# A macaron block with routed feed-forward: the class arithmetic of its sort moved to GpSimd, the sort's steps dealt out evenly over the tiles, and the counting matmuls put behind the last pair

## The chip, the cores and the metric

The kernel runs on one core of a Trainium2 chip. The metric is the device time of one execution in microseconds (us). Engines are named as the profile names them: PE (TensorE), ACT (ScalarE), DVE (VectorE), POOL (GpSimd), SP (SyncE, which here only starts transfers). PEld is the weight load of a matmul.

## The reference

The block is feed-forward, recurrence, feed-forward, each added to its input (cut to what matters):

```python
x = x + 0.5 * ffn(layernorm(x), W1, b1, W2, b2)
x = x + mixer(layernorm(x), W_toP, ..., W_fromP)      # projections and a scan over t
x = x + 0.5 * ffn(layernorm(x), W1, b1, W2, b2)

def ffn(x, W1, b1, W2, b2):                           # 8 experts, hidden 128 -> 512 -> 128
    h = mod(x[:, :2].sum(axis=1).astype(int32), 8)    # the class of a row
    for e in range(8):
        w = ((h == e) | (mod(h + 1, 8) == e)) / 2
        acc += w[:, None] * (maximum(x @ W1[e] + b1[e], 0) @ W2[e] + b2[e])
```

x has 16 sequences of 512 rows with 128 columns in float32, so 8192 rows. Each row uses two neighbouring experts, given by its class.

## The kernel before

**Tiles.** A feed-forward pass sorts the 8192 rows by class and works in 36 tiles of 256 rows, each gathered from DRAM by two indirect transfers (POOL, line 575) and scattered back by two (line 583). A *pure* tile holds one class; a *mixed* tile has two halves with classes of their own. `layout(j)` gives the order: `LEAD` pure tiles first, then mixed and pure by turns. Per tile PE does layer 1 (lines 877 to 879, each product as high and low halves in float16) and layer 2 (lines 895 and 897) of the tile before; ACT makes the high halves (`hhi`, line 703; `xhi`, line 709); DVE makes the low halves (`hlo`, line 1423, twice; `xlo`, line 1417), adds the bias row to the gathered rows (`residual`, line 1437, two instructions) and collects the result (`collect`, lines 1444 and 1447). PE's layer 1 of the next tile waits for that tile's `xlo`.

**The sort in two parts.** So that tiles can begin early, the first 48 of 64 row columns are sorted ahead of the pass and the last 16 inside it, between the tiles. Each part runs on DVE: row statistics (`bn_stats`), `moments` and `class_sum`, `classify` (a one-hot `oh` per class), then `count` on PE (lines 817 and 818), `ranks`, `assign_first` or `assign_rest` (arithmetic on 8 numbers, one per class, that ends in `code8`; `look_up` spreads it to the rows), `one_hots`, `select` on PE (line 831, 16 matmuls a group), `route` (writes `places`, the gather's indices) and `tables`. Inside a pass the helper `between(j, STEPS, ...)` takes up to 6 steps of the sort at two places of each tile, after the first `hlo` and after `collect`; a step ends at a `yield`. A stage must be done by its last tile (`all_of_it`).

**The order of the work.** Every engine runs its own list in the order written; semaphores join them. SP starts the loads in the order X (6 chunks), W1, W2, b2, `rows` (normalised rows for the gather), X (2 chunks), b1. Ahead of the first pass, PE and ACT also scale and split the 8 experts' W1 (`w_times` line 805, `w_less` line 810, `w_high`, `w_low`) and ACT sums the squares of W2 (line 686); the scale found from that goes through POOL back to ACT (line 692). The mixer runs over 8 pairs of sequences `q`; `add_out(q)` (line 1514) adds its result to X and takes the statistics of the new rows (line 1493). In its loop, at `q == NPAIR - 2`, DVE runs `own_classes(2)` and `classify(0, 48)` for the second pass, and PE has `count(3, ...)` there.

Of the kernel before, what the change touches and what calls it, by code (L numbers as in the profile page):

```python
# [22 lines left out]
P = 128  # L23
# [3 lines left out]
def macaron_kernel(nc, x, W_toP, W_U, W_F, W_V, W_lam, B_mat, C_mat, W_fromP, W1, b1, W2, b2, out):  # L27
# [17 lines left out]
    LEAD = PURE - (MIXED - 1)  # L45
# [10 lines left out]
    EARLY = 6  # L56
# [7 lines left out]
    with ExitStack() as ctx:  # L64
# [77 lines left out]
        n8 = sb("n8", [P, E])  # L142
        n8_i = sb("n8_i", [P, E], I32)
        p8 = sb("p8", [P, E])
        w8 = sb("w8", [P, E])
        u8 = sb("u8", [P, E])
        whole1 = sb("whole1", [P, E + 1])
        whole2 = sb("whole2", [P, E + 1])
        parts = sb("parts", [P, E + 1])
        code8 = sb("code8", [P, E])  # L150
# [73 lines left out]
        b1_hi = sem("b1_hi")  # L224
# [214 lines left out]
        STEPS = 6  # L439
        COUNT_AT = (3, 3)  # L440
        SELECT_AT = ((6, 7, 8, 9), (6, 7, 8, 9))

        @block.sync
        def _(sp):
# [7 lines left out]
            sp.dma_start(w1r[:], W1.rearrange("e d f -> d e f")).then_inc(w_in[0], 16)  # L452
            sp.dma_start(w2r[:], W2.rearrange("e (c p) d -> p e c d", p=P)).then_inc(w_in[2], 16)
# [10 lines left out]
            for c in range(FIRST[0] // XC, NX):  # L464
                load_x(c)
# [25 lines left out]
        def _(pool):  # L491
# [52 lines left out]
            pool.wait_ge(b1_hi, 2)  # L544
            g.tensor_tensor(b1l[:], b1f[:], b1h[:], ALU.subtract).then_inc(b1_lo, 1)
            pool.wait_ge(sum_in, 2)
# [82 lines left out]
        def _(act):  # L629
# [39 lines left out]
            nc.scalar.activation(b1h[:], b1r[:], ACT.Identity, scale=scl[0:E, 0:1]).then_inc(b1_hi, 1)  # L669
            nc.scalar.activation(b1f[:], b1r[:], ACT.Identity, scale=scl[0:E, 0:1]).then_inc(b1_hi, 1)  # L670
# [111 lines left out]
        def _(pe):  # L782
# [54 lines left out]
            def first_sort():  # L837
# [4 lines left out]
                warm(8, 0)  # L842
# [5 lines left out]
                w_less(EARLY - 2)  # L848
                w_less(EARLY - 1)
                for g in range(FIRST[0] // GRP):  # L850
                    if g == FIRST[0] // GRP - 1:
                        pe.wait_ge(sq_done, 2)
                        nc.tensor.matmul(ps[:, 6, 2:3], ones[:], sq[:, 2:3], start=True, stop=True,
                                         skip_group_check=True).then_inc(sum_pe, 1)
                    select(0, g)
# [746 lines left out]
```

## Time and profile before

| what | value |
|---|---|
| median of 3 runs | 618.48 us (616.67 to 619.98) |
| the profiled execution's own time | 618.32 us |
| its span | 616.5 us |
| PE busy | 522.9 us (85%) |
| DVE busy | 457.2 us (74%) |
| POOL busy | 314.5 us (51%) |
| ACT busy | 296.2 us (48%) |
| chain that ended last | PE 61%, DVE 22%, ACT 6% |

Read the table from the top: the profiled execution lies within the runs, 1.8 us of its time lie outside the span, and no engine is busy throughout. The stages have different limits: the head (0 to 54 us), the first pass (54 to 273), the mixer (273 to 361) and the second sort ahead of its pass (361 to 389), the second pass (389 to 608).

### The profile page before, as it was taken

Reading aid. Unit: us, or ns where it says so; the run is one execution under the profiler, and the core shown is the slowest. Engines: PE = TensorE matmul, PEld = TensorE weight load, DVE = VectorE, ACT = ScalarE, POOL = GpSimd, SP = SyncE. Lnnn points to the kernel's source line nnn. Section 1 sums busy time; section 2 is a strip of 40 time slices with the busy share of each in tenths; the row PEclk is TensorE's granted clock in tenths of the full one; section 3 lists DMA queues with packets and bytes.
Section 4 is the critical chain, followed back from the end, with each engine's and each line's share of the span. In section 5 each row is a group of like instructions: output and inputs, shape, how many; then the busy total and the mean of one; then the engine's idle time right before and its main releaser. Section 6 shows DMA issues by size and latency. Waiting matters only on the chain.

```text
span 616.5 us, 16284 instructions
## 1 busy us (share of the span) xinstructions
PE 522.9 (85%) x5367; PEld 441.8 (72%) x5367; DVE 457.2 (74%) x1191; ACT 296.2 (48%) x494; POOL 314.5 (51%) x379
## 2 busy tenths in 40 slices
PE   0586996999999999965799388798799999999991
PEld 0243885998999999952466264587698999999981
DVE  6887898778777777756876659589778777777771
ACT  2585352445555555522988110554344555555540
POOL 3128263647777767640016201646365777777642
PEclk9978898999999999997999787999899999999996
DMA  9961211112221112109003510241011221112200
GB/s 244 351 221 41 92 41 31 36 36 48 54 46 50 45 37 55 45 21 250 23 2 70 120 19 5 49 97 45 27 42 35 54 54 47 50 43 44 47 31 10
DMA packets 37852, 40.99 MB, mean 66 GB/s; under 512 B 5813, under 2 KB 30731, under 8 KB 37266
## 3 DMA queue, kind: packets, MB, share of 16 engines
q1 hardware_dynamic: 27698, 21.65, 12.7%
q0 software_dynamic: 9088, 17.87, 11.4%
q8 instruction: 52, 0.85, 0.6%
q10 hardware_dynamic: 992, 0.44, 0.3%
q14 instruction: 22, 0.18, 0.1%
HBM read 23.00 MB, written 17.83 MB: 66 GB/s over the span
## 4 chain that ended last, share of the span: by engine, by line
PE 61%; DVE 22%; ACT 6%; issue 4%; DMA 3%; SPq 1%; POOL 1%; DVEq 1%; POOLq 0%; ACTq 0%
PE ps L895 16%; PE ps L877 9%; PE ps L879 9%; PE ps L878 9%; PE ps L897 8%; DVE hlo L1423 5%; PE ps L913 2%; PE ps L797 2%; PE ps L831 2%; ACT hhi L703 2%; DVE bn L1493 1%; DMA X<-in_L_attn_x 1%; SPq L447 1%; DVE X L1514 1%; DMA X<-x1d 1%
## 5 line engine op out<-in xcount | busy, mean ns | idle before, releaser
L703 ACT ACTIVATE hhi<-ps 128x1024 f16<-128x1024 f32 x144 | 145.8, 1013 | 208.4 <-PE ps L879 208.4
L1423 DVE SCALAR_TENSOR_TENSOR hlo<-ps,hhi 128x1024 f16<-128x1024 f32 x144 | 173.9, 1208 | 85.8 <-ACT hhi L703 85.6
L575 POOL DMA_INDIRECT G<-rows,places x142 | 141.7, 998 | 133.2 <-PE ps L879 47.7
L895 PE MATMUL ps<-w2s,hhi 128*128 x1136 | 203.8, 274 | 0.1
L897 PE MATMUL ps<-w2s,hlo 128*128 x1136 | 196.1, 220 | 0.0
L877 PE MATMUL ps<-xhi,w1s 128*128 128x128 f16 (+1 forms) x736 | 169.9, 251 | 23.1 <-DVE xlo L1417 21.9
L879 PE MATMUL ps<-xhi,w1s 128*128 128x128 f16 (+1 forms) x736 | 169.7, 251 | 0.0
L878 PE MATMUL ps<-xlo,w1s 128*128 128x128 f16 (+1 forms) x736 | 169.6, 251 | 0.0
L895 PEld LDWEIGHTS ps<-w2s,hhi 128*128 128x128 f16 x1136 | 111.7, 98 | 12.6 <-issue 0.2
L897 PEld LDWEIGHTS ps<-w2s,hlo 128*128 128x128 f16 x1136 | 111.7, 98 | 1.4
L877 PEld LDWEIGHTS ps<-xhi,w1s 128*128 x736 | 72.6, 99 | 33.3 <-issue 27.7
L583 POOL DMA_INDIRECT x1d<-O,places x71 | 72.2, 1017 | 37.8 <-issue 22.7
L583 POOL DMA_INDIRECT out<-O,places x71 | 72.1, 1015 | 38.0 <-issue 24.7
L879 PEld LDWEIGHTS ps<-xhi,w1s 128*128 x736 | 72.6, 99 | 5.5
L717 ACT ACTIVATE xn<-G 128x127 f32<-128x127 f32 x142 | 62.0, 490 | 29.9 <-DMA G<-rows,places 29.9
L878 PEld LDWEIGHTS ps<-xlo,w1s 128*128 x736 | 72.7, 99 | 3.7
L797 PE MATMUL ps<-ones_row,ones 128*128 128x512 f16 x109 | 31.9, 457 | 10.2 <-DMA X<-x1d 9.5
L1437 DVE TENSOR_TENSOR O<-G,b2t 128x128 f32<-128x128 f32 x142 | 34.9, 286 | 2.6 <-issue 2.2
L1444 DVE SCALAR_TENSOR_TENSOR O<-ps,scl_i,O 128x256 f32<-128x256 f32 x72 | 33.9, 471 | 3.7 <-PE ps L897 3.7
L1447 DVE SCALAR_TENSOR_TENSOR O<-ps,scl_i,O 128x256 f32<-128x256 f32 x72 | 34.6, 480 | 2.5
L1417 DVE TENSOR_TENSOR xlo<-ps,xhi 128x256 f16<-128x256 f32 x72 | 29.6, 411 | 6.9 <-ACT xhi L709 6.9
L797 PEld LDWEIGHTS ps<-ones_row,ones 128*128 128x128 f16 x109 | 12.2, 115 | 26.6 <-issue 18.3
(263 smaller groups left out, 539.8 us busy)
## 6 DMA issues: line engine op xcount, KB each, us to landing
rows<-X SPq DMA_DIRECT2D x5, 1040.0 KB, 7.0
X<-in_L_attn_x SPq DMA_DIRECT2D x8, 512.0 KB, 8.7
X<-x1d SPq DMA_DIRECT2D x8, 512.0 KB, 7.2
rows<-X SPq DMA_DIRECT2D x1, 3120.0 KB, 12.7
G<-rows,places POOLq DMA_INDIRECT x142, 2.6
w1r<-in_L_ffn_W SPq DMA_DIRECT2D x1, 2048.0 KB, 9.0
x1d<-O,places POOLq DMA_INDIRECT x71, 2.3
out<-O,places POOLq DMA_INDIRECT x71, 2.3
```

The costliest lines, as they stand in the source:

```text
L575: nc.gpsimd.indirect_dma_start(out=G[tile.slot][:, s, :], out_offset=None, in_=src, in_offset=bass.IndirectOffsetOnAxis(ap=places[:, tile. ...
L583: nc.gpsimd.indirect_dma_start(out=dst, out_offset=bass.IndirectOffsetOnAxis(ap=places[:, tile.at, SUB + s:SUB + s + 1], axis=0), in_=O[ti ...
L703: nc.scalar.activation(hhi[tile.k][e][:, :, 0:tile.cols], H[e][:, :, 0:tile.cols], ACT.Relu).then_inc(hi_done[e], 1)
L717: ins = nc.scalar.activation(xn[tile.k][:, s, 0:D - 1], g[:, s, 0:D - 1], ACT.Identity, bias=g[:, s, D:D + 1], scale=g[:, s, D + 1:D + 2])
L797: nc.tensor.matmul(ps[:, bank, :], ones16[:], ones_row[:], start=True, stop=True)
L877: nc.tensor.matmul(o, hi, xhi[tile.k][:, tok], start=True, stop=False)
L878: nc.tensor.matmul(o, hi, xlo[tile.k][:, tok], start=False, stop=False)
L879: ins = nc.tensor.matmul(o, lo, xhi[tile.k][:, tok], start=False, stop=True)
L895: nc.tensor.matmul(Y[tile.k][:, s, :], hhi[tile.k][e][:, c, tok], w, start=first, stop=False, skip_group_check=True)
L897: ins = nc.tensor.matmul(Y[tile.k][:, s, 0:P], hlo[tile.k][e][:, c, tok], wh, start=False, stop=(e == 1 and c == CH - 1), skip_group_check ...
L1423: v.scalar_tensor_tensor(out=hlo[tile.k][e][:, :, c], in0=H[e][:, :, c], scalar=0.0, in1=hhi[tile.k][e][:, :, c], op0=ALU.max, op1=ALU.sub ...
L1437: ins = v.tensor_tensor(O[tile.slot][:, s, :], G[tile.slot][:, s, 0:D], b2v[:, bass.ds(at[0 if tile.pure else s], D)], ALU.add)
```

## The change

- `assign_first` and `assign_rest` lose their arithmetic on 8 classes. POOL does it (`codes_first`, `codes_rest`) with the scan over classes replaced by three shifted additions; DVE signals `counted` and waits for `coded` ahead of `look_up`. In a pass, `codes_rest` stands in POOL's list ahead of the gather of tile 6 + 4 (first pass) or 5 + 4 (second).
- Steps carry a cost (`yield 4`); `between` deals 4 units at each of the two places of a tile and carries what is over. The last part of the sort is spread over more tiles: counting after tile 4 or 3 as before 3, all four `select` groups after tile 12 or 11, where they stood after tiles 7 to 10, one each. 17 pure tiles lead, not 15. The second half's one-hot of the rank (`slots_of`) is made before the codes are there.
- Statistics of the last 16 columns move: 11 of 16 in the first sort ahead of the pass; those of the mixer's last two pairs out of `add_out`, 12 behind `tables` and 4 behind the first `xlo`.
- In the mixer `classify(0, 48)` runs behind the scan of the last pair, and `count(3, ...)` stands behind PE's loop.
- In the head, X's last two chunks are loaded ahead of W2; W1's 8 experts are all split ahead of the last `select`; POOL scales b1 and adds b2 earlier; `warm` has 6 matmuls, not 8.
- `residual` of a pure tile is one instruction.

```diff
-    LEAD = PURE - (MIXED - 1)
+    LATE = "MPMPMMPMPMPMMPMPMPM"
+    LEAD = NJ - len(LATE)
-    EARLY = 6
+    EARLY = 4
...
-        STEPS = 6
-        COUNT_AT = (3, 3)
-        SELECT_AT = ((6, 7, 8, 9), (6, 7, 8, 9))
+        STEPS = 4, 4
+        COUNT_AT = (4, 3)
+        CODES_AT = (6, 5)
+        SELECT_AT = (12, 11)
...
             sp.dma_start(w1r[:], W1.rearrange("e d f -> d e f")).then_inc(w_in[0], 16)
+            for c in range(FIRST[0] // XC, NX):
+                load_x(c)
             sp.dma_start(w2r[:], W2.rearrange("e (c p) d -> p e c d", p=P)).then_inc(w_in[2], 16)
...
             sp.dma_start(*rows_of(0, FIRST[0])).then_inc(rows_first[0], 16)
-            for c in range(FIRST[0] // XC, NX):
-                load_x(c)
...
+            def whole_of(out, src, less, by):
+                link(g.tensor_scalar(k8[:, 0], src, less, by, ALU.add, ALU.mult))
+                link(g.tensor_scalar(out, k8[:, 0], ROUND, -ROUND, ALU.add, ALU.add))
+            def summed(out, src):
+                link(g.tensor_tensor(z[3][:, own], src[:, own], src[:, after], ALU.add))
+                link(g.tensor_tensor(z[4][:, own], z[3][:, own], z[3][:, E - 2:2 * E - 2], ALU.add))
+                link(g.tensor_tensor(out[:, own], z[4][:, own], z[4][:, E - 4:2 * E - 4], ALU.add))
+            def codes_first(r):
+                pool.wait_ge(counted, 1 + 2 * r)
+                whole_of(z[5][:, own], n8[:, 0], 0.5 - FT / 2, 1.0 / FT)
+                summed(z[0], z[5])
...
+                g.tensor_tensor(code8[:, 0], k8[:, 3], k8[:, 2], ALU.add).then_inc(coded, 1)
+            def codes_rest(r):
+                pool.wait_ge(counted, 2 + 2 * r)
...
+                g.tensor_tensor(code8[:, 1], k8[:, 9], k8[:, 6], ALU.add).then_inc(coded, 1)
+            codes_first(0)
...
                 for j in range(NJ):
                     tile = Tile(r, j)
+                    if j == CODES_AT[r]:
+                        codes_rest(r)
...
+            w_both(0, EARLY)
             act.wait_ge(w_in[2], 16)
             nc.scalar.activation(w2s[:, :, :, 0:P], w2r[:], ACT.Square, accum_out=sq[:, 2:3]).then_inc(sq_done, 1)
+            w_both(EARLY, E - 2)
             act.wait_ge(sum_pe, 2)
             nc.scalar.activation(sums[:, 2:3], ps[:, 6, 2:3], ACT.Copy).then_inc(sum_in, 1)
+            w_both(E - 2, E)
             act.wait_ge(scale_ready, 2)
...
                 if q >= 1:
                     out_s(q - 1)
-                if q == NPAIR - 2:
-                    count(3, 0, FIRST[1])
+            count(3, 0, FIRST[1])
             out_x(NPAIR - 1)
...
+                dve.wait_ge(coded, 2 + 2 * r)
+                yield from look_up(1, NT)
...
-                stages = [(0, COUNT_AT[r] - 1, rest_classes(r)), (COUNT_AT[r] + 1, min(SELECT_AT[r]) - 1, rest_ranks(r))]
-                stages += [(SELECT_AT[r][g], SELECT_AT[r][g], one_hots(2 * r + 1, g)) for g in range(NT // GRP)]
-                stages += [(max(SELECT_AT[r]) + 2, max(SELECT_AT[r]) + 3, rest_routes(r))]
+                stages = [(0, COUNT_AT[r] - 1, early_part()), (COUNT_AT[r] + 1, SELECT_AT[r] - 1, middle_part()),
+                          (SELECT_AT[r] + 1, REST_AT[r] - 1, rest_routes(r))]
+                owed = [0.0]
                 def between(j, n, all_of_it):
                     for start, end, steps in stages:
                         if start <= j <= end:
-                            for k, _ in enumerate(steps):
-                                if k + 1 >= n and not (all_of_it and j == end):
+                            owed[0] += n
+                            while owed[0] > 0 or (all_of_it and j == end):
+                                cost = next(steps, -1)
+                                if cost == -1:
+                                    owed[0] = min(owed[0], 0.0)
                                     break
+                                owed[0] -= cost or 1
...
+                    if q >= NPAIR - 2:
+                        continue
                     if tiles is None:
                         dve.wait_ge(mx2, 2 * q + h + 1)
                         all_of(stats3(q, h))
...
+                if q == NPAIR - 1:
+                    run(classify(0, FIRST[1]))
...
-                    run(classify(0, FIRST[1]))
             run(ranks(3, 0, FIRST[1]))
+            run(slots_of(2, 0))
             run(assign_first(1))
```

Where the order of instructions moves, at three places. First, PE at the mixer's last pair: lines 817/818 (now 870/871) are the count of the second sort, lines 988 to 997 (now 1044 to 1053) the last pair's products. Before:

```order
L973 MATMUL ps<-m,w1r 128x128 x8
L817 MATMUL ps<-oh,after 128x384
L818 MATMUL ps<-oh,ones 128x384
L988 MATMUL ps<-w2r,wA 128x512
L989 MATMUL ps<-w2r,wB 128x512
L964 MATMUL ps<-m,w2r 128x128 x8
L997 MATMUL ps<-w1r,wL 128x512
```

With the change, the same place of PE's list:

```order
L1044 MATMUL ps<-w2r,wA 128x512
L1045 MATMUL ps<-w2r,wB 128x512
L1020 MATMUL ps<-m,w2r 128x128 x8
L1053 MATMUL ps<-w1r,wL 128x512
L1029 MATMUL ps<-m,w1r 128x128 x8
L870 MATMUL ps<-oh,after 128x384
L871 MATMUL ps<-oh,ones 128x384
```

The count has moved from ahead of the last pair's products to behind them.

Second, DVE in the first pass, from one `xlo` to the first `hlo` behind it, in the tile that follows the count. Before:

```order
L1106 SCALAR_TENSOR_TENSOR cum<-fresh,ps 128x128
L1111 TENSOR_TENSOR posv<-cum,ps 128x128
L1117 TENSOR_TENSOR posv<-posv,n 128x128
L1120 TENSOR_TENSOR n<-n,cum 128x8
L1121 TENSOR_TENSOR posv<-posv,oh 128x128
L1124 TENSOR_REDUCE rank<-posv 128x16
L1127 CAST q_i<-rank 128x16
L1417 TENSOR_TENSOR xlo<-ps,xhi 128x256
L321 TENSOR_LOAD tab_b
L1437 ISA
L1437 TENSOR_TENSOR O<-G,b2t 128x128 x2
L1423 SCALAR_TENSOR_TENSOR hlo<-ps,hhi 128x1024
```

With the change:

```order
L1159 SCALAR_TENSOR_TENSOR cum<-fresh,ps 128x128
L1167 TENSOR_TENSOR n<-n,cum 128x8
L1168 TENSOR_TENSOR posv<-cum,ps 128x128
L1417 TENSOR_TENSOR xlo<-ps,xhi 128x256
L321 TENSOR_LOAD tab_b
L1437 ISA
L1437 TENSOR_TENSOR O<-G,b2t 128x256
L1423 SCALAR_TENSOR_TENSOR hlo<-ps,hhi 128x1024
```

Three instructions of the sort stand ahead of `xlo` where seven stood, and the class totals `n`, for which POOL waits, come second.

Third, PE in the head: line 805 (now 858) scales an expert of W1, line 810 (now 863) takes its low half, line 831 (now 884) selects rows for the gather, line 853 (now 907) sums W2's squares. Before:

```order
L810 MATMUL ps<-w1s,minus 128x512 x3
L831 MATMUL ps<-onehot_a,onehot_b 128x34 x32
L853 MATMUL ps<-sq,ones 128x1
L831 MATMUL ps<-onehot_a,onehot_b 128x34 x16
L805 MATMUL ps<-w1r,fold 128x512 x2
L810 MATMUL ps<-w1s,minus 128x512 x2
L797 MATMUL ps<-ones_row,ones 128x512 x12
```

With the change:

```order
L884 MATMUL ps<-onehot_a,onehot_b 128x34 x16
L863 MATMUL ps<-w1s,minus 128x512
L907 MATMUL ps<-sq,ones 128x1
L863 MATMUL ps<-w1s,minus 128x512
L858 MATMUL ps<-w1r,fold 128x512 x2
L884 MATMUL ps<-onehot_a,onehot_b 128x34 x16
L863 MATMUL ps<-w1s,minus 128x512 x2
L884 MATMUL ps<-onehot_a,onehot_b 128x34 x16
L850 MATMUL ps<-ones_row,ones 128x512 x12
```

The last group of the selection now stands behind the last experts of W1, not ahead of them.

## Rows read from the trace of the kernel before

**Rows 1.** Page, costliest groups: busy, mean ns of one | idle before, releaser.
```profile
L877 PE MATMUL ps<-xhi,w1s 128*128 128x128 f16 (+1 forms) x736 | 169.9, 251 | 23.1 <-DVE xlo L1417 21.9
```

**Rows 2.** DVE timeline, `xlo` of single tiles: start, us, instruction.
```profile
54.13 0.42 DVE L1417 TENSOR_TENSOR xlo<-ps,xhi 128x256 f16<-128x256 f32 x1 [3.45 <-ACT xhi L709]
...
154.43 0.41 DVE L1417 TENSOR_TENSOR xlo<-ps,xhi 128x256 f16<-128x256 f32 x1
...
159.94 0.41 DVE L1417 TENSOR_TENSOR xlo<-ps,xhi 128x256 f16<-128x256 f32 x1
...
388.88 0.42 DVE L1417 TENSOR_TENSOR xlo<-ps,xhi 128x256 f16<-128x256 f32 x1 [3.48 <-ACT xhi L709]
...
485.42 0.41 DVE L1417 TENSOR_TENSOR xlo<-ps,xhi 128x256 f16<-128x256 f32 x1
```

**Rows 3.** Windows: us, busy of PE, PEld, DVE, ACT, POOL; PE clock; DMA share; GB/s.
```profile
154.43:159.94 5.51, 5.51 (x80) 5.25 (x79) 4.06 (x9) 3.08 (x5) 4.21 (x5) 1.00 0.20 52
87.19:94.02 6.83, 5.66 (x58) 4.89 (x58) 6.27 (x23) 3.08 (x5) 4.51 (x5) 1.00 0.17 47
40.00:45.00 5.00, 3.76 (x21) 2.69 (x22) 2.49 (x7) 3.42 (x5) 2.55 (x7) 0.50 0.06 13
```

**Rows 4.** Chain that ended last, 70 to 125 us: one group of the selection.
```profile
111.71 1.21 PE ps L831 x16
```

**Rows 5.** DVE timeline, first pass: first and last operation of `assign_rest`'s class arithmetic.
```profile
90.72 0.29 DVE L1195 CAST n_i<-n 128x8 int32<-128x8 f32 x1
...
98.09 0.17 DVE L1243 SCALAR_TENSOR_TENSOR code<-p,n 128x8 f32<-128x8 f32 x1
```

**Rows 6.** POOL and DVE timelines: small operations on POOL, one beside a DVE scan.
```profile
334.34 0.22 POOL L346 TENSOR_TENSOR l_v<-l_y,l_b 128x16 f32<-128x16 f32 x1
334.65 0.26 POOL L344 TENSOR_SCALAR l_c<-l_c 128x16 f32<-128x16 f32 x1
...
321.40 1.24 POOL L344 TENSOR_SCALAR l_c<-l_c 128x16 f32<-128x16 f32 x1
...
321.38 1.22 DVE L1549 TENSOR_TENSOR_SCAN w1r<-w1r 128x512 f32<-128x512 f32 x1
```

**Rows 7.** PE timeline at the mixer's last pair.
```profile
341.53 1.16 PE L973 MATMUL ps<-m,w1r 64*128 64x128 f32 x16
352.85 0.50 PE L817 MATMUL ps<-oh,after 128*128 128x384 f16 x1 [10.16 <-DVE oh L1098]
```

**Rows 8.** DVE timeline from there to the second pass's gather indices.
```profile
346.66 0.18 DVE L353 TENSOR_TENSOR l_m<-bn 128x16 f32<-128x16 f32 x1
...
350.73 0.19 DVE L1077 TENSOR_SCALAR c_b<-cls_s 128x48 f32<-128x48 f32 x1
...
360.35 1.23 DVE L1549 TENSOR_TENSOR_SCAN w1r<-w1r 128x512 f32<-128x512 f32 x1 [7.56 <-ACT w1r L775]
...
362.19 0.87 DVE L1493 BATCH_NORM_STATS2 bn<-X 128x6 f32<-128x128 f32 x4
...
364.48 0.93 DVE L1106 TENSOR_TENSOR_SCAN cum<-fresh,ps 128x384 f32<-128x384 f16 x1
```

**Rows 9.** POOL, ACT and PE timelines at the second pass's start.
```profile
382.78 1.30 POOL L575 DMA_INDIRECT G<-rows,places  x1 [38.62 <-DVE places L1307]
...
387.00 0.88 ACT L717 ACTIVATE xn<-G 128x127 f32<-128x127 f32 x2 [26.68 <-DMA G<-rows,places]
...
379.19 7.80 PE L797 MATMUL ps<-ones_row,ones 128*128 128x512 f16 x24
```

**Rows 10.** ACT, PE and POOL timelines in the head.
```profile
37.48 3.62 ACT L686 ACTIVATE w2s<-w2r 128x4096 f16<-128x4096 f32 x1
...
42.79 3.67 PE L805 MATMUL ps<-w1r,fold 128*128 128x512 f32 x4
...
46.26 1.23 POOL L575 DMA_INDIRECT G<-rows,places  x1 [0.18 <-issue]
```

More of the change, by code:

```diff
@@ L141, in macaron_kernel @@
         gone = sb("gone", [P, NT])
[L142 to L150, printed above, removed]
+        n8 = sb("n8", [P, 2, E])
+        k8 = sb("k8", [P, 12, E])
+        z16 = sb("z16", [P, 7, 2 * E])
+        whole1, whole2, parts = (z16[:, i, E - 1:2 * E] for i in range(3))
+        code8 = sb("code8", [P, 2, E])
         pairs8 = sb("pairs8", [P, E])
@@ L542, in _ @@
             power(c1).then_inc(scale_ready, 1)
-            pool.wait_ge(b1_hi, 2)
+            ROUND = 1.5 * 2.0 ** 23
+            z = [z16[:, i, :] for i in range(7)]
+            own, after = slice(E, 2 * E), slice(E - 1, 2 * E - 1)
+            def whole_of(out, src, less, by):
[5 more added lines that the diff above has]
+                link(g.tensor_tensor(out[:, own], z[4][:, own], z[4][:, E - 4:2 * E - 4], ALU.add))
@@ L1238, in assign_rest @@
-                yield
-                ch.wait()
-                ch.mark(v.tensor_tensor(n8[:], n8[:], u8[:], ALU.add))
-                yield
-                ch.wait()
-                ch.mark(v.scalar_tensor_tensor(out=code8[:], in0=p8[:], scalar=16384.0, in1=n8[:], op0=ALU.mult, op1=ALU.add))
-                yield
-                ch.wait()
-                yield from look_up(NT)
+                s = slice(0, FIRST[r])
+                dve.wait_ge(coded, 2 + 2 * r)
+                yield from look_up(1, NT)
@@ L1392, in rest_ranks @@
                 yield from ranks(2 + 2 * r, FIRST[r], NT)
+                for g in range(NT // GRP):
+                    yield from slots_of(2 * r + 1, g)
                 yield from assign_rest(r)
@@ L1397, in rest_routes, with some @@
                 yield from tables(2 * r + 1)
+            def some(steps, n):
+                for cost in steps:
+                    n -= cost or 1
+                    if n <= 0:
+                        break
+            late_stats = [rest_stats(0), rest_stats(1)]
             run(classify(0, FIRST[0]))
+            some(late_stats[0], 4)
             run(ranks(1, 0, FIRST[0]))
+            dve.wait_ge(iota_ready, 1)
+            run(slots_of(0, 0))
             run(assign_first(0))
-            dve.wait_ge(iota_ready, 1)
-            for g in range(FIRST[0] // GRP):
+            run(one_hots(0, 0))
+            for g in range(1, FIRST[0] // GRP):
+                run(slots_of(0, g))
                 run(one_hots(0, g))
+            some(late_stats[0], 11)
             run(route(0))
@@ L1576, in _ @@
             run(tables(2))
+            some(late_stats[1], 16)
             ffn(1)
```

251 lines of the change are left out of this document (112 added, 139 removed).

## The prediction

> **What bounds the kernel now.** I began with the page's groups of instructions, because they say what each engine waited for. PE is busy 85% of the span; its largest wait is the one ahead of layer 1 for `xlo` on DVE, 21.9 us in all [rows 1]. Next I took the start of single `xlo` instructions from DVE's timeline, which dates the tiles [rows 2]. Without steps of the sort a tile takes 159.94 - 154.43 = 5.51 us, and there PE is busy 5.51 of 5.51 us, DVE 4.06, POOL 4.21 [rows 2, 3]: the pass is bound by PE. The first 15 tiles are not. They take 154.43 - 54.13 = 100.30 us in the first pass and 485.42 - 388.88 = 96.54 in the second, against 15 x 5.51 = 82.65 [rows 2]. A tile that holds 12 sort steps takes 6.83 us, and DVE is busy 6.27 of them [rows 3]: there DVE is the bound. Last, the timelines at the mixer's end. PE finishes a product at 342.7 and then stands for 10.16 us, because the count is next in its list and waits for the one-hot `oh` of `classify` on DVE; the last pair's products stand behind that count [rows 7]. So the kernel has three places where PE waits for DVE: early tiles of both passes, and the mixer's end.
>
> 0.5% of this time is 3.1 us, about what a measurement of this kernel can tell from no change. The sum is made against the profiled execution, 618.32 us (616.5 in the span), 0.16 under the median.
>
> **(a) The mixer's end and the second sort: -11.8 us.** Before, DVE ends `own_classes` at 350.73, where `classify` begins, and `classify` runs until PE's count at 352.85, so 2.12 us [rows 7, 8]. The scan of the last pair then starts only at 360.35, 7.5 us behind, since PE and ACT make its input after the count; with two additions to X and 8 row statistics (two of 4, about 0.81 each) `ranks` starts at 364.48 [rows 8]. With the change PE goes on at 342.7, and the same 7.5 us put the scan's input at about 350.2, before DVE is through with `own_classes`. DVE then does the scan (1.23), `classify` (2.12) and the two additions (364.48 - 360.35 - 1.14 - 1.62 = 1.37): 350.73 + 4.72 = 355.45 instead of 364.48, so -9.0. From `ranks` to the gather it was 382.78 - 364.48 = 18.30 us [rows 8, 9]. Out of that go 8 class operations of about 0.19 (1.5 us) and the other 8 statistics (1.6 us); the moved ones are dealt behind `tables` and the first `xlo`, where PE is warming or working. That is -12.1, if POOL's answer is in time: 10 operations at a pitch of 0.31 (334.65 - 334.34) are 3.1 us [rows 6], and DVE has 3.7 us of its own ahead of `look_up` (the positions, the rank and one one-hot). The gather's landing 4.2 us later is not alone: PE's 24 warming matmuls end at 379.19 + 7.80 = 386.99, as `xn` starts at 387.00 [rows 9]. Both move with the selection; I give back 0.3 for a slower clock in the warming. Bounds: -12.6, and -10 if warming takes 2 us longer.
>
> **(b) First 15 tiles of the second pass: -7.1 us.** What PE cannot avoid is 82.65, plus four groups of selection at 1.21 each [rows 4], 4.85. The rest depends on DVE. In a tile with 12 steps, 6.83 - 4.06 = 2.77 us go to the steps, 0.23 a step [rows 3]. The change deals 8 units a tile: 8 x 0.23 + 4.06, less about 0.1 for the single `residual`, gives 5.8 against 5.51, 0.3 late. I count about 93 units in the list, 11.6 tiles, so 3.5 us a pass, at most 4.2 with slips; and none if DVE's lead in the two tiles without steps absorbs it. I take 2.3, past the middle, since 0.3 us is 5% of a tile and the cost of a step is a mean. The first interval is 0.4 shorter by fewer statistics in it. 82.65 + 4.85 + 2.3 - 0.4 = 89.4 against 96.54.
>
> What makes the steps fewer is the class arithmetic, which leaves DVE: 18 operations from 90.72 to 98.09, 0.16 to 0.29 each, 3.4 us a pass [rows 5]. On POOL it is 22 operations, 19 linked, 19 x 0.31 + 3 x 0.22 = 6.5 us. DVE asks for it some 12 units, 1.45 tiles, after it gave the totals: 8.0 us of cover. The gathers behind it in POOL's list are 6.5 us late; they stand four tiles ahead (22 us), land within 4.2, and POOL wins back 5.51 - 4.21 = 1.30 a tile [rows 3], so nothing waits for them.
>
> **(c) First 15 tiles of the first pass: -9.7 us.** The same 82.65 + 4.85 + 2.3. Three statistics stand ahead of the second `xlo` where twelve stood (-0.6). PE comes out of the head at a granted clock of 0.50 [rows 3], the lower of its two levels (1.2 of 2.4 GHz), with fewer warming matmuls; for that I add 1.4, a quarter of a tile, between 0 and 2.8. 90.6 against 100.30.
>
> **(d) The head: +1.5 us.** The last group of the selection moves behind four scaling matmuls of experts 6 and 7, which took 3.67 us at the lower clock [rows 3, 10]. With their low halves the route, and the gather that stood at 46.26, come up to 3 us later; at the full clock they come at the same time. ACT's sum of squares (37.48, 3.62 us [rows 10]) starts earlier, as it no longer waits for the split of two experts; X's two chunks ahead of W2 delay its landing, still under that start. DVE leaves its part of the critical path. Bounds -0.9 and +3. POOL's work on b1 and b2 lies ahead of the route, which it used to follow: nothing.
>
> Sum: -11.8 - 7.1 - 9.7 + 1.5 = -27.1, so **591.2 us**.
>
> **The rivals.**
> *Codes come late.* POOL's prices are from a quiet stretch. Beside a DVE scan the same operation took 1.24 us instead of 0.26 and ended with it [rows 6]. If the mix costs 0.6 an operation, 22 x 0.6 = 13.2 less 8.0 leaves 5.2 late in each pass, and PE, with DVE late by as much, follows: 591.2 + 10.4 = 601.6. The Trainium skill, page "SBUF — State Buffer", section "Who interferes with whom", states that GpSimd shares a port pair with DVE's second input under an exclusive lock, so that one waits until the other's instruction ends. The trace agrees, 1.24 beside a scan of 1.22 [rows 6]. By it I would put the 6.5 us at about 9.0, 1.0 late a pass, and the time at 593. Chance 0.12.
>
> *The class arithmetic on POOL becomes the bound* (the other side). At 1.24 us for every operation [rows 6] 22 take 27.3, 19.3 past the cover, twice 38.6; and the 10 ahead of each pass 12.4, 8.7 past their cover in the second: about 638. Against it: DVE's steps of 0.2 to 0.5 us are mostly shorter than that scan, and it is idle a quarter of the time. It decides from about 0.98 us an operation, where 2 x (22 x 0.98 - 8.0) = 27.1. Chance 0.05, of which 0.02 near no change.
>
> *The spreading does nothing*: DVE's work is the same, each pass is as late as before, and only (a) and (d) remain: 618.3 - 11.8 + 1.5 = 608. For it: PE waits for whatever is late last. Against it: DVE's total in 15 tiles, 15 x 4.0 + 93 x 0.23 = 81, is under PE's 87.5. Chance 0.05.
>
> *Half of the mixer's gain* if DVE, busy in the whole of PE's gap [rows 7, 8], receives the scan's input later than 350.7: 597. Chance 0.08.
>
> **How the numbers follow.** The forecast has 0.70. Its own best end (no lag, full clock, head -0.9) is about 583, its worst (lag 4.2 twice, head +3, mixer -10) about 598. The late codes take the range to 602; outside lie the spread's rival (0.05), the slower one (0.05), the part of the late codes beyond 0.6 an operation (about 0.05) and a tail of the forecast, below 0.2 in all. Faster by over 0.5%: 0.95; within: 0.02; slower: 0.03.
>
> **What would show it.** (a) PE's wait of 10.16 ahead of the count is gone, `ranks` starts near 355.5 plus the shift of the passes, and from the last pair's end to the first `xlo` it is 12 us less. (b, c) The wait for `xlo` falls from 21.9 to about 5, and `xlo` intervals in the first 15 tiles are 5.5 to 6.0. POOL's class operations show 0.2 to 0.3 us and DVE's `look_up` does not wait for them. (d) The first `xlo` is at about 55.6. It is wrong if `look_up` waits for POOL, if PE waits for `xlo` just as long, or if tiles 9 to 12 wait for gathers.

## The result, and the profile after

The changed kernel takes 594.51 us (median of 4 runs, 593.97 to 595.11); beside it the kernel before took 619.23 us. The ratio is 0.9608, with a 95% interval of 0.9576 to 0.9640. The forecast was 591.2 us in a range of 583 to 602: the sign is right, the time lies in the range, and the gain is 24.4 us (profiled execution 593.97 against 618.32) where 27.1 were forecast.

The span went from 616.5 to 592.0 us. First the same group of the page as [rows 1], with its new line number: busy, mean ns of one | idle before, releaser.

```profile
L933 PE MATMUL ps<-xhi,w1s 128*128 128x256 f16 (+1 forms) x736 | 171.3, 251 | 6.2 <-DVE xlo L1417 4.8
```

PE's wait for `xlo` fell from 21.9 to 4.8 us. To date the stages, DVE's timeline of the changed kernel (start, us, instruction): the first `xlo` of each pass, the sixteenth, and the last.

```profile
55.30 0.42 DVE L1417 TENSOR_TENSOR xlo<-ps,xhi 128x256 f16<-128x256 f32 x1 [1.99 <-ACT xhi L762]
...
145.75 0.41 DVE L1417 TENSOR_TENSOR xlo<-ps,xhi 128x256 f16<-128x256 f32 x1
...
257.29 0.28 DVE L1417 TENSOR_TENSOR xlo<-ps,xhi 128x128 f16<-128x128 f32 x1
...
369.56 0.42 DVE L1417 TENSOR_TENSOR xlo<-ps,xhi 128x256 f16<-128x256 f32 x1 [1.25 <-ACT xhi L762]
...
458.94 0.42 DVE L1417 TENSOR_TENSOR xlo<-ps,xhi 128x256 f16<-128x256 f32 x1
...
571.17 0.28 DVE L1417 TENSOR_TENSOR xlo<-ps,xhi 128x128 f16<-128x128 f32 x1
```

The kernel before has its first and sixteenth in [rows 2]; its last of each pass are these:

```profile
264.68 0.28 DVE L1417 TENSOR_TENSOR xlo<-ps,xhi 128x128 f16<-128x128 f32 x1
...
595.64 0.28 DVE L1417 TENSOR_TENSOR xlo<-ps,xhi 128x128 f16<-128x128 f32 x1
```

Differences between these starts give the whole account:

| stretch | before | after | change | forecast |
|---|---|---|---|---|
| (d) head, to the first `xlo` | 54.13 | 55.30 | +1.2 | +1.5 |
| (c) first 15 tiles, pass 1 | 100.30 | 90.45 | -9.9 | -9.7 |
| the other 20 tiles of pass 1 | 110.25 | 111.54 | +1.3 | none |
| (a) last `xlo` to the next pass's first | 124.20 | 112.27 | -11.9 | -11.8 |
| (b) first 15 tiles, pass 2 | 96.54 | 89.38 | -7.2 | -7.1 |
| the other 20 tiles of pass 2 | 110.22 | 112.23 | +2.0 | none |

The four terms that were forecast came out within 0.3 us each. That is closer than executions agree: two kernels below whose instructions are the same up to tile 17 (`mixed_run` and `fixed_addr`) have their first `xlo` at 55.04 and 55.73 us and take 91.52 and 91.94 us for the first 15 tiles of the first pass. What is missing is a stretch that had no term: the tiles behind the sixteenth, where the kernel before ran at 5.51 us a tile. Two windows there, columns as in [rows 3]: from the `xlo` of tile 22 of the first pass to that of tile 23, and on to that of tile 24.

```profile
183.04:188.84 5.80, 5.80 (x82) 5.39 (x79) 4.06 (x9) 3.08 (x5) 4.28 (x6) 1.00 0.17 50
188.84:195.19 6.35, 6.28 (x69) 5.43 (x68) 4.05 (x9) 3.08 (x5) 4.01 (x5) 1.00 0.12 34
```

They are 5.80 and 6.35 us at the full clock (2.4 GHz), with DVE busy for no more than 4.06 us, as in a tile of 5.51. The next two intervals are 5.57 and 5.62, so 1.3 us are lost. The same happens seven tiles on and at both places of the second pass, four times 1.3 = 5.2 us. These are the two places in `LATE` with "MM", two mixed tiles side by side (21 and 22, 28 and 29); the alternation before had none. (The rows of the table show less, 3.3, since `xlo` had fallen behind PE during the selection and makes that up there: the two intervals behind tile 15 of the first pass are 4.84 and 4.90 us; in the second pass one is short, 5.00.)

One more loss lies inside the first 15 tiles, and no term had it. Before, the selection stood behind four tiles, 16 matmuls (128x37) each; now all 64 stand in a row. Windows, columns as in [rows 3]: the kernel before over its four groups of the first pass, then the changed kernel at the end of the row in the first and in the second pass.

```profile
110.00:135.00 25.00, 25.00 (x280) 23.31 (x278) 18.21 (x33) 10.94 (x17) 14.90 (x15) 1.00 0.15 41
```

```profile
130.00:135.00 5.00, 5.00 (x54) 4.47 (x52) 0.41 (x1) 0.00 (x0) 3.78 (x5) 0.75 0.19 53
440.00:445.00 5.00, 5.00 (x38) 4.07 (x36) 0.07 (x1) 1.12 (x2) 3.98 (x4) 0.50 0.19 53
```

PE's granted clock falls from 1.00 to 0.75 and 0.50 there, though PE shows as busy. The tile behind the row takes PE 6.91 and 8.09 us from its first product of layer 1 to the next tile's (133.18 to 140.09 and 441.10 to 449.19), where the tiles shortly ahead take 5.48: 1.4 and 2.6 us. It varies between executions: in the second pass of `b2_later` (experiment 8) the same tile took 5.66 us at a clock of 1.00. No run deals the four groups out again, so what that would bring is not shown.

The mixer's end, on PE and DVE, with the first gather on POOL:

```profile
340.34 1.16 PE L1029 MATMUL ps<-m,w1r 64*128 64x128 f32 x16
346.69 0.50 PE L870 MATMUL ps<-oh,after 128*128 128x384 f16 x1 [5.19 <-DVE oh L1151]
...
347.87 0.95 DVE L1159 TENSOR_TENSOR_SCAN cum<-fresh,ps 128x384 f32<-128x384 f16 x1
...
363.50 1.32 POOL L625 DMA_INDIRECT G<-rows,places  x1 [10.27 <-DVE places L1291]
```

From the last `xlo` to `ranks` it is now 347.87 - 257.29 = 90.58 us, before 364.48 - 264.68 = 99.80 [rows 8]: -9.2, forecast -9.0. From `ranks` to the gather 15.63 against 18.30: -2.7, forecast -3.1. PE still waits 5.19 us for the one-hot `oh`, but only the last pair's products of the output stand behind it; the scan's input is made ahead.

The class arithmetic in the first pass: its first, its longest and its last operation on POOL, and DVE beside it.

```profile
91.80 0.26 POOL L551 TENSOR_SCALAR k<-n 128x8 f32<-128x8 f32 x1
...
97.47 1.24 POOL L587 TENSOR_SCALAR k<-k 128x8 f32<-128x8 f32 x1
...
99.08 0.20 POOL L590 TENSOR_TENSOR code<-k 128x8 f32<-128x8 f32 x1
...
97.42 1.23 DVE L1266 TENSOR_TENSOR onehot_b<-iota_rep,b_h 128x2048 f16<-128x2048 f16 x1
98.56 1.22 DVE L1423 SCALAR_TENSOR_TENSOR hlo<-ps,hhi 128x1024 f16<-128x1024 f32 x1
99.70 0.68 DVE L1194 TENSOR_TENSOR posv<-oh,code 128x512 f32<-128x512 f16 x1
```

POOL takes 7.5 us (91.80 to 99.28), one operation being stretched to 1.24 beside a DVE instruction of 1.23, as in [rows 6]. DVE takes up `look_up` at 99.70 and waits for nothing, with 0.4 us to spare.

### The profile page after: what moved, and what is told of

It reads as the page before. It is cut to its first block, busy times and chain, and to the rows that moved or that the text cites. A ratio compares the mean times of both kernels' runs of the same rounds, so it can differ in the third digit from the quotient of the medians.

```text
span 592.0 us, 16239 instructions
## 1 busy us (share of the span) xinstructions
PE 521.4 (88%) x5365; PEld 441.6 (75%) x5365; DVE 443.8 (75%) x1087; ACT 296.1 (50%) x492; POOL 339.1 (57%) x445
## 3 DMA queue, kind: packets, MB, share of 16 engines
q0 software_dynamic: 9088, 17.87, 11.3%
## 4 chain that ended last, share of the span: by engine, by line
PE 66%; DVE 16%; issue 4%; DMA 4%; ACT 3%; POOL 3%; SPq 1%; DVEq 0%; POOLq 0%; ACTq 0%
PE ps L951 19%; PE ps L933 10%; PE ps L935 10%; PE ps L934 10%; PE ps L953 9%; DVE hlo L1423 3%; PE ps L969 2%; PE ps L884 2%; POOL G L625 1%; DMA X<-in_L_attn_x 1%; SPq L448 1%; DVE X L1533 1%; ACT hhi L756 1%; DMA G<-rows,places 1%; DMA X<-x1d 1%
## 5 line engine op out<-in xcount | busy, mean ns | idle before, releaser
L625 POOL DMA_INDIRECT G<-rows,places x142 | 144.3, 1017 | 77.2 <-issue 43.8
L933 PE MATMUL ps<-xhi,w1s 128*128 128x256 f16 (+1 forms) x736 | 171.3, 251 | 6.2 <-DVE xlo L1417 4.8
L935 PE MATMUL ps<-xhi,w1s 128*128 128x256 f16 (+1 forms) x736 | 171.3, 250 | 0.0
L934 PE MATMUL ps<-xlo,w1s 128*128 128x256 f16 (+1 forms) x736 | 170.9, 250 | 0.0
L850 PE MATMUL ps<-ones_row,ones 128*128 128x512 f16 x107 | 30.2, 443 | 9.6 <-DMA X<-x1d 9.6
L969 PE MATMUL ps<-ident,xn 128*128 128x128 f32 x142 | 28.2, 280 | 4.6 <-ACT xn L770 4.6
```

The source lines that it names most:

```text
L625: nc.gpsimd.indirect_dma_start(out=G[tile.slot][:, s, :], out_offset=None, in_=src, in_offset=bass.IndirectOffsetOnAxis(ap=places[:, tile. ...
L850: nc.tensor.matmul(ps[:, bank, :], ones16[:], ones_row[:], start=True, stop=True)
L933: nc.tensor.matmul(o, hi, xhi[tile.k][:, tok], start=True, stop=False)
L934: nc.tensor.matmul(o, hi, xlo[tile.k][:, tok], start=False, stop=False)
L935: ins = nc.tensor.matmul(o, lo, xhi[tile.k][:, tok], start=False, stop=True)
L969: ins = nc.tensor.transpose(XTP[:, s * P:(s + 1) * P], xn[(tile + 1).k][:, s, :], ident[:])
```

## The experiments

All are compared with the kernel before, run beside them; ratios carry 95% intervals.

**1. Only the mixer's part** (`mixer_only`), in the kernel before:

```diff
+                if q == NPAIR - 1:
+                    run(classify(0, FIRST[1]))
...
-                    run(classify(0, FIRST[1]))
...
-                if q == NPAIR - 2:
-                    count(3, 0, FIRST[1])
+            count(3, 0, FIRST[1])
             out_x(NPAIR - 1)
```

> The kernel before, with only the counting matmuls behind PE's loop and classify behind the last pair's scan; everything else as before. Theory (term a, its first half): PE no longer waits for DVE ahead of the last pair's products, so ranks starts 9.0 us earlier, less the 1.6 us of statistics that stay in add_out (the same 1.6 us stood there before, so they cancel): about 609.5 to 610.5. Rival: the scan's input comes no earlier because DVE is busy throughout PE's gap; then half of it or less, 614 or more.

610.95 us against 618.62 (0.9872, 0.9844 to 0.9901): -7.7. Its `ranks` on DVE:

```profile
355.59 0.94 DVE L1105 TENSOR_TENSOR_SCAN cum<-fresh,ps 128x384 f32<-128x384 f16 x1
```

The first pass ended 1.4 us earlier here (last `xlo` at 263.28), so `ranks` moved by 7.5 us. That is the forecast's 9.0 less the 1.6 us of row statistics, which this kernel keeps and the change moves away; the expectation was wrong to say that they cancel. The mechanism is shown for this half of (a): two moved calls are worth almost a third of the gain.

**2. Mixed tiles in a row** (`mixed_run`), the suspected loss enlarged:

```diff
-    LATE = "MPMPMMPMPMPMMPMPMPM"
+    LATE = "MMMMMMMMMMPPPPPPPPM"
```

> The changed kernel with ten mixed tiles in a row after the 17 leading pure ones, then eight pure tiles, then the last half tile. In the changed kernel the two places in each pass where two mixed tiles stand side by side are 1.3 us longer than the 5.51 us a tile give. Theory: a mixed tile has more PE instructions with computed weight addresses than PE can issue in 5.51 us, and a pure tile between two of them gives the time back; nine such neighbours in place of two then cost 9 x 1.3 = 11.7 instead of 2.6 us in a pass, 18 us more in all: 610 to 616. Rival: the loss sits at these two tiles for another reason (a late gather or scatter): within 2 us of 594.5.

614.73 us (0.9941, 0.9918 to 0.9965): 20 us above the change, at the upper end of the theory. A window within the row, and PE's timeline there:

```profile
184.00:191.00 7.00, 7.00 (x86) 5.87 (x83) 4.21 (x8) 3.08 (x5) 4.13 (x5) 1.00 0.12 32
```

```profile
177.29 0.23 PE L933 MATMUL ps<-xhi,w1s 128*128 128x128 f16 x1
177.35 0.22 PE L934 MATMUL ps<-xlo,w1s 128*128 128x128 f16 x1
177.41 0.23 PE L935 MATMUL ps<-xhi,w1s 128*128 128x128 f16 x1
177.54 0.23 PE L933 MATMUL ps<-xhi,w1s 128*128 128x128 f16 x1
177.60 0.22 PE L934 MATMUL ps<-xlo,w1s 128*128 128x128 f16 x1
```

A mixed tile among its like takes 7.0 us, and no other engine is busy for more than 4.21 of them. Three products start within 0.25 us (177.29 to 177.54) with a pause ahead of line 933. In the first of two mixed neighbours of the changed kernel they start within 0.17:

```profile
182.19 0.22 PE L933 MATMUL ps<-xhi,w1s 128*128 128x128 f16 x1
182.25 0.22 PE L934 MATMUL ps<-xlo,w1s 128*128 128x128 f16 x1
182.30 0.22 PE L935 MATMUL ps<-xhi,w1s 128*128 128x128 f16 x1
182.36 0.22 PE L933 MATMUL ps<-xhi,w1s 128*128 128x128 f16 x1
```

**3. The same with fixed weight addresses** (`fixed_addr`):

```diff
-                            hi = w1v[:, bass.ds(at + c * P, P)]
-                            lo = w1v[:, bass.ds(at + DFF + c * P, P)]
+                            if not tile.pure:
+                                at = (2 * s + e) * WS
+                                hi, lo = w1v[:, at + c * P:at + (c + 1) * P], w1v[:, at + DFF + c * P:at + DFF + (c + 1) * P]
+                            else:
+                                hi = w1v[:, bass.ds(at + c * P, P)]
+                                lo = w1v[:, bass.ds(at + DFF + c * P, P)]
```

> The run with ten mixed tiles in a row, in which layer 1 of a mixed tile takes its weights from places fixed in the program, not from places computed at run time by the tile's classes. So mixed tiles use the wrong experts in layer 1; the number and the shapes of the matmuls, the weight loads and all waits stay. Theory: the 7.0 us of a mixed tile among its like is PE's own instruction stream, which has a computed address for each weight load; with fixed ones a mixed tile takes 5.5 us wherever it stands, and the time falls from 614.7 to 588 to 592. Rival: the weight loads or the half-width matmuls themselves need 7.0 us: within 2 us of 614.7.

588.49 us (0.9505, 0.9467 to 0.9542). The window in the row of mixed tiles:

```profile
184.00:189.50 5.50, 5.50 (x85) 5.31 (x83) 4.01 (x8) 3.04 (x6) 4.28 (x5) 1.00 0.13 34
```

As many matmuls and weight loads as in the 7.0 us above (85 and 83 against 86 and 83) now fit in 5.50. So neither the products nor the weight loads set the 7.0 us, but the addresses computed at run time in PE's own list. That a pure tile between two mixed ones gives PE time to get ahead, as it has half of layer 1's computed addresses, fits the 5.51 us of the alternation in the kernel before; how far ahead PE's list was read is in no row, so this stays a reading.

**4. Strict alternation, 16 tiles ahead** (`lead16`):

```diff
-    LATE = "MPMPMMPMPMPMMPMPMPM"
+    LATE = "MPMPMPMPMPMPMPMPMPMM"
-        SELECT_AT = (12, 11)
+        SELECT_AT = (11, 10)
```

> The changed kernel with 16 pure tiles leading instead of 17, mixed and pure tiles strictly by turns, and the one pair of mixed neighbours at the end of the pass, where the second is the half tile; the selection after tile 11 and 10 instead of 12 and 11. Theory: four pairs of neighbours at 1.3 us are gone, and the half tile at the end costs little: -4 to -5 us, 589.5 to 590.5. Rival: the steps of the sort have one tile less, so what is left over is forced out at the deadline and PE waits for DVE: gain of 2 us or less, or a loss.

590.07 us (0.9532, 0.9505 to 0.9559), 4.4 us below the change and with an interval apart from its own. From tile 16 on every interval of `xlo` is 5.50 to 5.52 us, the pair at the end included. This is the missing term of the prediction. With one tile less for the steps PE waits 5.4 us for `xlo` in all, against 4.8. The loss behind the selection stays: that tile takes 7.86 and 7.16 us here.

**5. The steps of the sort in fewer tiles** (`steps5`, `steps6`):

```diff
-        STEPS = 4, 4
+        STEPS = 5, 5
```

(6, 6 in the second.)

> The changed kernel with 5 units of sort steps at each of the two places of a tile instead of 4 (10 a tile), nothing else: the same steps, done in fewer tiles. Theory (evenness is what pays): at 8 units a tile DVE just keeps pace, PE waits for xlo 4.8 us in all; at 10 units a tile DVE needs about 4.0 + 10 x 0.19 = 5.9 of 5.51 us, 0.4 late in some nine tiles of each pass, so PE waits up to 3.7 us more a pass: 597 to 602. Rival: the amount of work decides, not its spread: 594.5 +- 1.

> The changed kernel with 6 units of sort steps at each place (12 a tile, the number of steps of the kernel before). Theory: 4.0 + 12 x 0.19 = 6.3 of 5.51 us, 0.8 late in some eight tiles, 6.2 us a pass, and the codes from POOL are asked for sooner, which adds up to 2 us a pass: 602 to 611. Rival: the amount of work decides: 594.5 +- 1.

602.63 us (0.9726, 0.9688 to 0.9765) and 602.39 us (0.9730, 0.9687 to 0.9773): 8 us each. PE's waits in the first and the second (us in total, times, longest us):

```profile
PE ps L933 <- DVE xlo L1417: 12.4, 18, 2.4
```

```profile
PE ps L933 <- DVE xlo L1417: 14.4, 15, 2.6
```

The same steps cost 8 us more when they stand closer: the wait for `xlo` rises from 4.8 to 12.4 and 14.4. That evenness pays is shown. The size law behind the expectations is not: 12 units a tile cost no more than 10 (which would fit late tiles that are later but fewer), and 10 cost a little more than was worked out. Up to 2.0 us of it in each run is not the spacing itself: DVE waits 1.0 us in each pass for POOL's codes, which it asks for sooner. With 12 units the first 15 tiles still take 9.1 us less than before in the two passes together (96.07 and 91.69 us); what of that is due to the statistics, the single `residual` or the order of the steps no run separates, and the class arithmetic adds nothing that can be seen (experiment 6).

**6. The class arithmetic back on DVE** (`codes_dve`), with 10 units a tile; `codes_first` and `codes_rest` become steps on DVE:

```diff
-                dve.wait_ge(coded, 2 + 2 * r)
+                yield from codes_rest(r)
```

> The changed kernel with the same class arithmetic issued by DVE as steps of the sort, not by POOL, and 10 units a tile so that the steps fit (compare with the run at 10 units and the codes on POOL). Theory: 22 operations of 0.21 more on DVE in a pass and 10 in each first part of the sort: 4.6 us a pass where DVE is behind, 1.7 at the second pass's start (2.1 less the 0.4 us that DVE now waits for POOL), up to 0.6 in the head: 5 to 11 us above the run at 10 units with the codes on POOL. Rival: PE hides DVE's steps anyway and POOL's contention with DVE is gone: within 2 us of that run.

605.52 us (0.9771, 0.9733 to 0.9810), 2.9 us above `steps5`; the intervals of the two overlap, though no run of either reaches into the other's (601.86 to 602.70 and 604.53 to 606.56). That lies under the theory and over the rival. In the profiles 1.8 us of it lie in the second sort, between the last `xlo` and the next first (113.73 against 111.89), as expected; pass 1 hardly differs (207.96 against 207.71). Pass 2 is 2.4 us longer, but not by DVE's steps: PE's wait for `xlo` is 11.9 us in all, against 12.4 in `steps5`. What differs is the clock, at the second tile (first window: this run, second: `steps5`) and behind the selection (0.50 from 453 to 458 us here, 0.80 from 450 to 455 there):

```profile
382.00:387.00 5.00, 4.05 (x25) 3.25 (x26) 3.70 (x12) 1.72 (x5) 2.24 (x4) 0.66 0.10 27
```

```profile
380.40:385.40 5.00, 4.04 (x41) 3.53 (x42) 4.46 (x14) 2.12 (x5) 3.12 (x4) 1.00 0.18 43
```

So the arithmetic on DVE is shown to cost 1.8 us at the second sort, not 5 to 11; inside the passes it costs nothing that can be seen, as the rival had it ("PE hides DVE's steps anyway").

**7. The class arithmetic twice on POOL** (`codes_twice`), the first round's result unused:

```diff
+                link(g.tensor_tensor(k8[:, 10], k8[:, 9], k8[:, 6], ALU.add))
+                whole_of(k8[:, 4], n8[:, 1], 0.5 - FT / 2, 1.0 / FT)
...
                 g.tensor_tensor(code8[:, 1], k8[:, 9], k8[:, 6], ALU.add).then_inc(coded, 1)
```

> The changed kernel with the in-pass class arithmetic on POOL done twice over (22 operations more in a pass, the first round's result unused). Theory: POOL had the codes 0.4 us ahead of DVE's look-up in each pass (99.28 against 99.70), so the second round makes look-up some 7.1 us late; xlo stands behind it on DVE, so PE waits 6 to 7 us in each pass and gets none of it back: 606 to 609. Rival: DVE's lead and later tiles take it up: under 598.

609.62 us (0.9838, 0.9799 to 0.9877): 15.1 us. What DVE and PE waited for (us in total, times, longest us):

```profile
DVE posv L1211 <- POOL code L607: 11.4, 2, 5.7
...
PE ps L950 <- DVE xlo L1434: 16.8, 7, 5.8
```

PE's wait for `xlo` grows by 12.0 us, where DVE's wait for POOL is 11.4; nothing takes it up later. The rest fits the clock: two windows of the first pass, during and behind PE's wait of 5.8 us (same columns as in [rows 3]),

```profile
105.00:110.00 5.00, 2.62 (x13) 1.96 (x14) 3.75 (x7) 0.00 (x0) 3.55 (x8) 0.50 0.09 23
110.00:115.00 5.00, 5.00 (x49) 4.45 (x48) 2.69 (x5) 3.08 (x5) 3.78 (x5) 0.86 0.14 43
```

have PE at a granted clock of 0.50, then 0.86, where the changed kernel has 1.00:

```profile
90.00:110.00 20.00, 20.00 (x212) 18.16 (x210) 19.00 (x37) 11.21 (x19) 15.42 (x32) 1.00 0.11 31
```

The cover of the codes ends at 0.4 us, and the waits beyond it cost more here than their length.

**8. POOL's b2 additions later** (`b2_later`):

```diff
-            pool.wait_ge(w_in[3], 16)
-            g.tensor_tensor(b2t[:, 0:E - 1, :], b2r[:, 0:E - 1, :], b2r[:, 1:E, :], ALU.add)
-            g.tensor_tensor(b2t[:, E - 1, :], b2r[:, E - 1, :], b2r[:, 0, :], ALU.add).then_inc(b2_sum, 1)
...
             power(c3).then_inc(scale_ready, 1)
+            pool.wait_ge(w_in[3], 16)
...
```

> The changed kernel with POOL's two additions that make b2t moved from the middle of the first sort to behind the scale of W2. Theory: in the head of the changed kernel a DVE multiplication of 128x544 took 3.43 us beside POOL's 2.07 us addition (0.43 alone), and PE stood 3.43 us for it; with POOL's addition gone from there the multiplication takes about 1.5 us or less, PE's wait shrinks by about 2 us, and the first xlo comes 1 to 2 us earlier: about 592.5 to 593.5. Rival: the last group of the selection is held by ACT's sum of squares and the experts behind it, whatever DVE does: no change, 594.5 +- 0.4.

594.07 us (0.9606, 0.9584 to 0.9629): no difference that can be measured. The contention is real all the same. In the changed kernel DVE and POOL stand like this:

```profile
35.95 3.43 DVE L1258 TENSOR_TENSOR onehot_a<-onehot_a,tokid 128x544 f16<-128x544 f16 x1
...
35.89 1.15 POOL L595 TENSOR_TENSOR b1l<-b1f,b1h 8x512 f16<-8x512 f32 x1
37.01 2.07 POOL L597 TENSOR_TENSOR b2t<-b2r 128x896 f32<-128x896 f32 x1
```

and with the additions moved:

```profile
35.70 1.39 DVE L1258 TENSOR_TENSOR onehot_a<-onehot_a,tokid 128x544 f16<-128x544 f16 x1
...
35.64 1.14 POOL L595 TENSOR_TENSOR b1l<-b1f,b1h 8x512 f16<-8x512 f32 x1
```

The DVE instruction ends 0.30 us behind the last POOL instruction in both (39.38 and 39.08; 37.09 and 36.78); alone it takes 0.44. PE's wait for it shrank from 3.43 to 0.8 us, but then PE stood for ACT, which sums the squares of W2 until 39.6. The rival's reading of the head holds.

The Trainium skill, page "SBUF — State Buffer", section "Who interferes with whom", has it that a DVE instruction with two inputs in SBUF and a GpSimd instruction that reads SBUF exclude each other, and that the one issued first keeps the ports until it ends. These rows agree, 3.43 against 0.44 us, and show it over two POOL instructions in succession.

**9. The head in the order of before** (`head_order`), the rest as changed:

```diff
-    EARLY = 4
+    EARLY = 6
...
-                warm(6, 0)
+                warm(8, 0)
...
-                select(0, 0)
-                w_less(EARLY)
...
+                for g in range(FIRST[0] // GRP):
...
+                    select(0, g)
+                for e in range(EARLY, E):
+                    w_times(e)
```

> The changed kernel with the order of PE and ACT in the head as in the kernel before: six experts of W1 split ahead of the sum of squares, the last group of the selection ahead of experts 6 and 7, eight warming matmuls. Loads and POOL stay as changed. Theory (term d): the first xlo was 1.2 us later for the last group's place behind four scaling matmuls; that comes back, but DVE, held up by POOL's b2 additions, and ACT, which splits two experts more ahead of the sum, take some of it: 593.3 to 594.5. Rival: the new order hides the sum of squares, and without it the head is longer: 595 to 597.

592.05 us (0.9553, 0.9524 to 0.9581), 2.5 below the change and more than the theory gave; the two intervals just touch. But the first `xlo` is no earlier (55.15 against 55.30). What the traces show of the gain, 1.2 us of it, is in the next tile: 4.86 us from the first `xlo` to the second, where the changed kernel has 6.02. The second `xlo` of the changed kernel, then the first two of this run:

```profile
61.32 0.41 DVE L1417 TENSOR_TENSOR xlo<-ps,xhi 128x256 f16<-128x256 f32 x1
```

```profile
55.15 0.42 DVE L1413 TENSOR_TENSOR xlo<-ps,xhi 128x256 f16<-128x256 f32 x1 [1.35 <-ACT xhi L761]
60.01 0.41 DVE L1413 TENSOR_TENSOR xlo<-ps,xhi 128x256 f16<-128x256 f32 x1
```

PE around the first tile of the changed kernel, and a window there:

```profile
47.08 2.76 PE L850 MATMUL ps<-ones_row,ones 128*128 128x512 f16 x12
54.12 0.66 PE L969 MATMUL ps<-ident,xn 128*128 128x128 f32 x2 [4.27 <-ACT xn L770]
```

```profile
55.00:60.00 5.00, 5.00 (x31) 3.25 (x29) 3.12 (x3) 3.32 (x6) 4.08 (x4) 0.76 0.16 43
```

and of this run:

```profile
49.58 2.76 PE L849 MATMUL ps<-ones_row,ones 128*128 128x512 f16 x12 [0.69 <-ACT w1s L728]
54.22 0.41 PE L965 MATMUL ps<-ident,xn 128*128 128x128 f32 x2 [1.87 <-ACT xn L769]
```

```profile
55.00:60.00 5.00, 3.72 (x30) 2.58 (x27) 4.40 (x6) 4.53 (x9) 4.29 (x3) 1.00 0.16 42
```

In the changed kernel the warming matmuls end at 49.84, PE stands for 4.27 us, and the first tile runs at a mean granted clock of 0.76; with the old order they come later, PE stands 1.87 us, and the clock is 1.00. So the new order brings the warming forward and loses it. The other runs fit: all ten traces with the new order have 6.00 to 7.07 us between the first two `xlo`, and the second one with the old order (`lead16_head`, below) has 4.86.

**10. The edits that helped, together.** `lead16_b2` is experiments 4 and 8; `lead16_head` is 4, 8 and 9.

> Both edits that helped, together: 16 leading pure tiles with mixed and pure by turns, and POOL's b2 additions behind the scale of W2. Theory: they touch different stages and add up: 590.1 - 0.4 = 589.7. Rival: the b2 edit's 0.4 us was no effect: 590.1.

> The three edits together: 16 leading tiles by turns, b2 later, head order of the kernel before. Theory: with b2 out of DVE's way the old order gives the full 1.2 us: 588.5 to 589. Rival: the old order costs 1 to 2 us: 591 to 592.

589.11 us (0.9501, 0.9469 to 0.9534), not to be told from `lead16` alone, so the b2 edit's effect stays open; and 587.79 us (0.9487, 0.9459 to 0.9515), the fastest of all and 6.7 us below the change: its interval lies below the change's. The first `xlo` there is at 54.14, ahead of every trace with the new order of the head (54.68 to 55.81), while the old order alone had 55.15. That fits the two edits acting together, but it is one execution of each.

## Why the prediction was right, and where it was off

- **What bounds the kernel.** Right. The three places where PE waited for DVE are the three where time was won.
- **(a)** Right in mechanism and size (-11.9 against -11.8); its first half is shown by experiment 1, and of the second half only the class arithmetic was moved by itself (1.8 us in experiment 6). Of its steps the 9.0 to `ranks` measured 9.2; of the 3.1 from there to the gather, 2.7 came, since POOL's codes were 0.4 us late (DVE waited for `code8` from POOL by that much); the 0.3 for a slower clock was not needed.
- **(b) and (c).** The sums are right (-7.2 and -9.9), the steps only in part. "I take 2.3" for late steps was too much: PE waited for `xlo` only four times, 1.83 and 2.20 us of the 4.8 at the second tile of each pass and 0.19 and 0.56 at two others, so the steps of the sort cost under a microsecond in all at 8 units a tile; the prediction's own other end ("none if DVE's lead ... absorbs it") came near. In the place of the 2.3 stood what the sum did not have: above all the clock behind the selection (1.4 us in the first pass, 2.6 in the second), then the wait of the second tile, and an `xlo` that was 1.3 and 0.5 us behind at the sixteenth. That these filled the 2.3 is luck. The 1.4 us for the clock at the first tile was about right: experiment 9 got 1.2 of it back between the first two `xlo`.
- **The class arithmetic.** "6.5 us" measured 7.5. The "8.0 us of cover" came out by two errors that cancel: DVE asked 11.3 us after it gave the totals (88.41 to 99.70), not 8.0, but POOL, busy with its transfers, started 3.4 us late (91.80), which left 7.9. So DVE waited for no code inside the passes, but by 0.4 us, not 1.5. That "nothing waits for them", the gathers behind it, holds for PE only: ACT stood 0.51 and 0.30 us for two of them in the first pass and 0.53 and 0.34 in the second, the sign that the prediction named ("if tiles 9 to 12 wait for gathers"), too short to reach PE. Experiment 7 shows that the rival "codes late" was near: its price, once past the cover, is paid in full by PE. And that the arithmetic left DVE, which the prediction gives as what makes the steps of a pass fewer, was worth nothing that can be seen inside the passes (experiment 6, at 10 units a tile).
- **(d)** Right in sum (+1.2 against +1.5, though traces with the same head differ by 1.1 us; the gather came at 48.68, 2.4 later). "POOL's work on b1 and b2 ...: nothing" was wrong as a statement on DVE (3.43 us for an instruction of 0.44) and right for the time, because ACT ended last there (experiment 8).
- **What failed** is a term that was left out: the section on the change lists "17 pure tiles lead, not 15", and the sum has nothing for the order of the late tiles. Their list was read for what must be ready when, not for what stands beside what. Four pairs of mixed neighbours at 1.3 us are 5.2 us (experiments 2 to 4). With it the sum would have come to 596.4, 1.9 us above the measured time; as much is what `xlo` makes up behind the sixteenth tiles (5.2 less the 3.3 of the table), which the sum did not have either.
- **The rivals.** "The spreading does nothing" is refuted by experiment 5 (8 us), "half of the mixer's gain" by experiment 1 (`ranks` 7.5 us earlier). "The class arithmetic becomes the bound" did not come; POOL's operations took 0.20 to 0.39 us, but for one of 1.2 to 1.3 in each round. The estimate of 9.0 us by the port rule was 1.5 us over the measured 7.5, and its 1.0 us late a pass did not come.

## What to carry to other kernels

When a table that orders tiles changes, look at which kinds now stand next to each other, on each engine by itself: an engine that shows as busy may be short of instructions, and its own list is then the bound. Work that must run between other work is best dealt out so evenly that no stretch needs more than the bounding engine leaves; the same steps in fewer tiles cost 8 us here. Work moved to POOL is free only up to its cover, so read how much of that is left (0.4 us) before adding to it.

## What was not expected of the hardware

- A matmul stream with computed weight addresses ran at 7.0 us a tile where the same count of matmuls and weight loads with fixed addresses ran at 5.50, with PE shown as busy throughout (7.00 of 7.00 us). The page of the profile does not tell the two apart; the starts of single matmuls do.
- A DVE multiplication of 0.44 us took 3.43 us through two POOL instructions in a row.
- PE's granted clock over the first tile was 0.76 after it had stood for 4.27 us, and 1.00 after 1.87 us; in experiment 7 it was 0.50 after 5.8 us.
- PE's granted clock also fell while PE showed as busy: to 0.50 at the end of 64 selection matmuls (128x37) in a row, where 16 behind each of four tiles left it at 1.00. In the second pass of two other runs (`b2_later`, `mixed_run`) the same row left it at 1.00.
